# Six buffers in place of eight in the first mean stage, whole index lists, edge blocks, and two tiles of room before the gathers, in a four-layer graph network kernel

## The reference

```
q, k, v = x @ qW + qb, x @ kW + kb, x @ vW + vb
scores = sum(q[src] * k[dst]) / sqrt(16) + edge_attr @ eW + eb
out = segment_sum(v[src] * softmax_by_dst(scores), dst) @ oW + ob
x = layer_norm(x + out); h = gelu(layer_norm(x @ f1W + f1b)) @ f2W + f2b
x = layer_norm(x + h)
```

## Time and profile before

| | us |
|---|---|
| median of 3 runs | 6024.28 |
| lowest and highest run | 6012.01, 6027.09 |
| profiled execution, its own time | 6028.9 |
| its span in the trace | 6027.0 |

### The profile page before, as it was taken

How to read it: one execution, slowest core, us unless ns; L and a number is a source line. 1 busy time by engine, 2 the same in 40 slices (tenths; PEclk the granted TensorE clock), 3 DMA queues, 4 the chain that set the end, 5 groups by cost and what they waited for, 6 DMA issues and landing times. The chain is left out here.

```text
span 6027.0 us, 75672 instructions
## 1 busy us (share of the span) xinstructions
PE 4279.1 (71%) x16190; PEld 2524.1 (42%) x16190; DVE 4070.7 (68%) x13522; ACT 2924.8 (49%) x6388; POOL 3629.7 (60%) x3234
## 2 busy tenths in 40 slices
PE   6577759999997556546665679967996669836643
PEld 3244434444443333334443445534443334336643
DVE  6576659999997444457775676557665889836633
ACT  0466637777775010146665345534443446536643
POOL 4676558888885888735555660056104757855355
PEclk8788869999998777778887899988998899977877
DMA  6233323333332444456665675457545667757621
GB/s 214 66 85 80 73 70 99 99 99 99 99 99 78 62 62 63 54 141 196 193 190 162 185 211 146 131 160 214 164 141 147 176 159 211 197 162 227 183 78 54
DMA packets 767598, 802.43 MB, mean 133 GB/s; under 512 B 139632, under 2 KB 527800, under 8 KB 767018
## 3 DMA queue, kind: packets, MB, share of 16 engines
q1 hardware_dynamic: 405354, 393.44, 23.5%
q0 software_dynamic: 117504, 209.42, 15.0%
q10 hardware_dynamic: 244288, 194.72, 9.7%
HBM read 445.32 MB, written 351.92 MB: 132 GB/s over the span
## 5 line engine op out<-in xcount | busy, mean ns | idle before, releaser
L462 PE MATMUL gate_bank<-gate_ht,gate_whh 128*128 128x512 f32 x1764 | 874.6, 618 | 32.5 <-DVE gate_n L532 22.2
L925 POOL DMA_INDIRECT xh<-mean_xh,mean_pos_all x392 | 378.0, 964 | 349.0 <-DVE mean_xh L1027 158.9
L462 PEld LDWEIGHTS gate_bank<-gate_ht,gate_whh 128*128 128x128 f32 x1764 | 341.3, 202 | 413.0 <-issue 381.6
L2053 PE MATMUL back_ps_sums<-back_same,back_rows 128*128 128x512 f32 x400 | 289.5, 890 | 285.7 <-DMA back_rows<-x_a,back_idx 285.7
L151 POOL DMA_INDIRECT ffn_rows<-att_sums,ffn_idx x392 | 409.0, 1043 | 114.8 <-issue 106.3
L289 POOL DMA_INDIRECT gate_rows<-h_a,by_pos x200 | 195.8, 979 | 433.3 <-POOLq L117 327.3
L1494 PE MATMUL ffn_ps_f<-ffn_hg,ffn_f 128*128 128x512 f32 x784 | 407.1, 616 | 46.4 <-ACT ffn_hg L1671 46.4
L458 PE MATMUL gate_bank<-by_rank,gate_win 128*128 128x512 f32 x882 | 435.1, 593 | 0.0
L1487 PE MATMUL ffn_ps_u<-ffn_xs_t,ffn_up_w 128*128 128x512 f32 x784 | 387.2, 596 | 1.1 <-issue 1.1
L583 ACT ACTIVATE gate_z<-gate_bank,gate_b_rz 128x512 f32<-128x512 f32 x294 | 201.5, 686 | 351.0 <-PE gate_bank L462 221.0
L2034 POOL DMA_INDIRECT back<-back_out,back_dest x200 | 324.3, 1621 | 68.0 <-issue 60.1
(11 more groups left out here) (270 smaller groups left out, 11984.1 us busy)
## 6 DMA issues: line engine op xcount, KB each, us to landing
mean_x<-x_a SPq DMA_DIRECT2D x196, 256.0 KB
back<-blank ACTq DMA_DIRECT2D x99, 264.0 KB, 4.6
mean_rows<-back SPq DMA_DIRECT2D x98, 264.0 KB
hp<-mean_xh SPq DMA_DIRECT2D x98, 264.0 KB
gate_x<-xh SPq DMA_DIRECT2D x98, 264.0 KB
gate_hot<-hot_rows SPq DMA_DIRECT2D x100, 256.0 KB
ffn_x<-in_x_in SPq DMA_DIRECT2D x98, 256.0 KB
ffn_xr<-in_x_in SPq DMA_DIRECT2D x98, 256.0 KB
```

The source lines that it names most:

```text
L462: last = nc.tensor.matmul(bank_[:, :], whh[:, c * D:(c + 1) * D], ht[:, t.slot4, :], start=not inputs, stop=True)
L925: nc.gpsimd.indirect_dma_start(out=g["xh"][:, :], out_offset=bass.IndirectOffsetOnAxis(ap=pos_all[:, t.n, j:j + 1], axis=0), in_=xh[:, t.n ...
L2053: last = nc.tensor.matmul(ps_sums[t.slot][:, :], rows[:, t.slot4, j, :], same[:, t.slot, j, :], start=j == 0, stop=j == J - 1)
```

## The change

- First mean stage: the buffers `xh`, and the semaphores `scattered` and `h_stored`, go from 8 to FINISHED = 6. ACT's write of tile t waits for the scatter of tile t-6 (before: t-8).
- `SegmentSums.gather`, where the stage doesn't carry sums over (gate1, gate2 and mean3), and the gathers of attention: POOL waits for the use of tile t-2 (before: t-4), so two tiles of rows can be ahead of PE and not four. The buffers stay four.
- `gated_layer`: `hn` has four buffers (before: two), and the transposes of hn, what follows them on ACT and the stores come at item 3 (before: 2). In gate2 DVE's out and statistics come at item 3, rstd and shifts at 6 (5), apply, y's store and the scatter at 7 (6), the read back at 6 (5). Each layer's loops are one step longer.
- attention: SP loads the indices from a new input `edge_blocks` in which edge 128·j + p of a tile lies at partition p; turned rows are written to contiguous columns, L1206 reads contiguous columns of att, and `att_sums` is stored in pieces of 512 bytes in place of 2 KB.
- feed-forward: the whole list `ptr_dst` (98 tiles, 128 partitions, pieces of 16 bytes) is loaded once, first on SP's queue, in place of 98 loads; POOL's add a = rows + x goes to DVE, after z and ahead of the statistics; POOL's order in a step is gathers, xb, pow; and xh becomes `scalar_tensor_tensor` with the inverse root broadcast along the row as a second SBUF tensor, in place of `tensor_scalar`.

```
 SegmentSums.gather
-        wait(pool, self.summed, t.n - 3)
+        wait(pool, self.summed, t.n - 3 if self.carries else t.n - 1)
 gated_layer
-        d, hn = (f.sb(s, [P, 2, SUPER]) for s in ("d", "hn"))
+        d, hn = f.sb("d", [P, 2, SUPER]), f.sb("hn", [P, 4, SUPER])
 SP
-                if final and (t := item_at(5)) and t.has:
+                if final and (t := item_at(6)) and t.has:
 POOL
-                if final and (t := item_at(5)):
+                if final and (t := item_at(6)):
                     ln.rstd(nc, pool, t, y_done)
-                if final and (t := item_at(6)) and t.has:
+                if final and (t := item_at(7)) and t.has:
 PE
-                if t := item_at(2):
+                if t := item_at(3):
                     wait(pe, h_done, t.n + 1)
                     wait(pe, out_done, t.n)
...
-            over_items(2, step)
+            over_items(3, step)
 DVE
-                    wait(dve, h_turned, t.n - 1)
+                    wait(dve, h_turned, t.n - 3)
...
-                if final and (t := item_at(2)):
+                if final and (t := item_at(3)):
                     wait(dve, h_turned, t.n + 1)
                     wait(dve, x_loaded[t.slot4], 16 * (t.u4 + 1))
 back_mean_pass
-        xh = f.sb("xh", [P, 8, J, XH])
+        xh = f.sb("xh", [P, FINISHED, J, XH])
...
-                    wait(act, scattered[t.n % 8], 64 * (t.n // 8))
-                    wait(act, y_turned, t.n - 7)
+                    wait(act, scattered[t.n % FINISHED], 64 * (t.n // FINISHED))
+                    wait(act, y_turned, t.n + 1 - FINISHED)
 attention_pass
-                                 nm_tile(g["by_dst"], t)).then_inc(idx_loaded[t.slot4], 16)
+                                 g["edge_blocks"][t.n]).then_inc(idx_loaded[t.slot4], 16)
...
-                    wait(pool, rows_turned, t.n - 3)
+                    wait(pool, rows_turned, t.n - 1)
...
-                        nc.tensor.transpose(edge_columns(ps_send[:, :])[:, j, :], send[:, t.slot4, j, :], g["ident"][:, :])
+                        nc.tensor.transpose(ps_send[:, j * P:(j + 1) * P], send[:, t.slot4, j, :], g["ident"][:, :])
...
-                        last = nc.tensor.matmul(ps_out[:, j * D:(j + 1) * D], edge_columns(att[:, t.slot, :])[:, j, :],
+                        last = nc.tensor.matmul(ps_out[:, j * D:(j + 1) * D], att[:, t.slot, j * P:(j + 1) * P],
...
-                    act.dma_start(nm_tile(g["att_sums"], t), out[:, t.slot, :]).then_inc(stored[t.slot], 16)
+                    act.dma_start(part_tile(g["att_sums"], t.n, 0, D),
+                                  out[:, t.slot, :].rearrange("p (j d) -> p j d", j=J)).then_inc(stored[t.slot], 16)
 ffn_pass
-        idx = f.sb("idx", [P, 4, J], I32)
+        idx = f.sb("idx", [P, NT, J], I32)
...
+            sp.dma_start(idx[:, :, :], whole_list(g["ptr_dst"])).then_inc(idx_loaded, 16)
...
-                    wait_alone(sp, gathered[t.slot4], 64 * t.u4)
-                    sp.dma_start(idx[:, t.slot4, :], list_tile(g["ptr_dst"], t)).then_inc(idx_loaded[t.slot4], 16)
...
-                if t := tile_at(2):
-                    wait(pool, gathered[t.slot4], 64 * (t.u4 + 1))
-                    wait(pool, x_loaded[t.slot4], 16 * (t.u4 + 1))
-                    wait(pool, xh_done, t.n - 3)
-                    nc.gpsimd.tensor_tensor(flat(a[:, t.slot4, :, :]), flat(rows[:, t.slot4, :, :]),
-                                            flat(x[:, t.slot4, :, :]), ALU.add).then_inc(a_done, 1)
...
-                        last = nc.vector.tensor_scalar(xh[:, t.slot4, j, :], a[:, t.slot4, j, :],
-                                                       mv[:, root_slot(t, LN1), LN1, j, 0:1], inverse(t, LN1)[:, j:j + 1],
-                                                       ALU.subtract, ALU.mult)
+                        last = nc.vector.scalar_tensor_tensor(
+                            xh[:, t.slot4, j, :], a[:, t.slot4, j, :], mv[:, root_slot(t, LN1), LN1, j, 0:1],
+                            inverse(t, LN1)[:, j:j + 1].broadcast_to([P, D]), ALU.subtract, ALU.mult)
...
+                if t := tile_at(2):
+                    wait(dve, gathered[t.slot4], 64 * (t.u4 + 1))
+                    wait(dve, x_loaded[t.slot4], 16 * (t.u4 + 1))
+                    wait(dve, xh_done, t.n - 3)
+                    nc.vector.tensor_tensor(flat(a[:, t.slot4, :, :]), flat(rows[:, t.slot4, :, :]),
+                                            flat(x[:, t.slot4, :, :]), ALU.add).then_inc(a_done, 1)
```

More of the change, by code:

```diff
@@ L420, in step @@
                                  ).then_inc(back_loaded[t.m % 4], 16)
-            over_items(5 if final else 0, step)
+            over_items(6 if final else 0, step)
             if initial:
@@ L584, in step @@
                                          bias=b_rz[:, 1:2]).then_inc(z_done, 1)
-                if not final and (t := item_at(2)):
+                if not final and (t := item_at(3)):
                     wait(act, h_turned, t.n + 1)
@@ L602, in step @@
                     nc.scalar.activation(ht[:, t.slot4, :], ps_in[:, :], ACT.Copy).then_inc(ht_made, 1)
-                if final and (t := item_at(6)):
+                if final and (t := item_at(7)):
                     wait(act, y_done, t.n + 1)
                     act.dma_start(part_tile(x_out, t.tile, 0, D), y[:, t.slot, :, :]).then_inc(stored[t.slot], 16)
-            over_items(6 if final else 2, step)
+            over_items(7 if final else 3, step)
             for b in range(2):
                 act.wait_ge(stored[b], 16 * (NT // 2))
-                if not final:
-                    act.wait_ge(ht_stored[b], 16 * (NT // 2))
+            if not final:
+                for b in range(4):
+                    act.wait_ge(ht_stored[b], 16 * ((NT - b + 3) // 4))
 class Turn:
@@ L1437, in step @@
             def step(tile_at):
-                if t := tile_at(2):
-                    wait(pool, gathered[t.slot4], 64 * (t.u4 + 1))
-                    wait(pool, x_loaded[t.slot4], 16 * (t.u4 + 1))
-                    wait(pool, xh_done, t.n - 3)
-                    nc.gpsimd.tensor_tensor(flat(a[:, t.slot4, :, :]), flat(rows[:, t.slot4, :, :]),
-                                            flat(x[:, t.slot4, :, :]), ALU.add).then_inc(a_done, 1)
+                if t := tile_at(0):
+                    if t.n == 0:
+                        pool.wait_ge(idx_loaded, 16)
+                    wait(pool, a_done, t.n - 3)
+                    pool.nop(nofuse=True)
+                    for j in range(J):
+                        nc.gpsimd.indirect_dma_start(
+                            out=rows[:, t.slot4, j, :], out_offset=None, in_=g["att_sums"][:, :],
+                            in_offset=bass.IndirectOffsetOnAxis(ap=idx[:, t.n, j:j + 1], axis=0)
+                        ).then_inc(gathered[t.slot4], 16)
                 if t := tile_at(10):
```

60 lines of the change are left out of this document (31 added, 29 removed).

## The result

The changed kernel took 5861.08 us (median of 4 executions, 5828.97 to 5862.3) beside 6021.82 for the kernel before (6012.01 to 6027.09): a ratio of 0.9722, with a 95% interval of 0.9686 to 0.9758. The gain is 160.7 us where I had forecast 85; 5861 is at the very edge of my range (5860 to 6018). The profiled execution took 5861.81, its span is 5860.0.

A forecast was written before the change was run, and what follows sets the result against it. No engine bounds the whole kernel; POOL's own work sets the feed-forward step of 10.74 us. Terms -92 + 7 + 0 - 5 + 4 + 0 + 0 = -86 take 6028.9 to 5942.9, forecast as 5939 for the median; range 5860 to 6018.

The forecast's parts named there:

- Feed-forward, the step: Feed-forward stage: POOL's step of 10.74 us falls to 9.8 with PE late next, -92 us over 98 steps.
- The chance that POOL's remaining add would hold xh: Feed-forward rival: the xb add holds DVE's xh or z, stage gains only 21 us, time 6010; chance 0.10.
- The start: Start of the feed-forward stage: the whole index list goes ahead of the weights, +7 us, between 0 and +14.5.
- Attention: Attention: two tiles of room are enough for gathers, 0; shorter weight loads 0, at best -50; lower PE clock at worst +35.
- Segment sums' room: gate1, gate2 and mean3: two tiles of room before the gathers change nothing, 0, bounds -20 to +30 us.
- Bigger gain, the rival: First mean stage or stages like it: less room breaks up POOL's trains, 84 us more gained, time 5855; chance 0.12.
- Gated layers: Gated layers: PE's wait for hn goes, -5 us; one more step of drain a layer, +4 for the three.
- Slower by late x loads: Last gated layer rival: x loads over 4.9 us delay ACT; loads from 7.0 us give over 6042; chance 0.09.
- First mean stage: First mean stage: six buffers for eight cost 0, as POOL scatters a tile about as soon as it is done.

The follow-up runs named there:

- e7: The changed kernel with xh by the old tensor_scalar form again: 5925.19 us, ratio 0.9824 to the kernel before.
- e8: The kernel before with the new form of xh alone, both adds still on POOL: 6009.92 us beside 6028.14, ratio 0.9979.
- e14: The kernel before with six buffers of finished rows in the first mean stage alone: 6029.27 us beside 6026.5, ratio 1.0.
- e12: The changed kernel with six buffers of x in the last gated layer: 5895.71 us beside 6064.17 for the kernel before, ratio 0.9709.
- e18: The changed kernel with three tiles of room in attention: 5485.45 us beside 5583.56 for the kernel before, ratio 0.9824.
- e15: The changed kernel with one tile of room before attention's gathers: 5944.37 us, ratio 0.9856 to the kernel before.

## Why the prediction was right and wrong

- **Feed-forward, the step: mechanism right, one number mis-sized.** POOL's work did set the step. I had its new value, 9.48, by plain subtraction, and took 9.8 because PE's busy time gave 9.78. Measured: 9.42. The step of the prediction that failed here is the one from an upper bound to a value: "PE is late next. I take 9.8". PE's 9.78 held time in which it was not at work: its share shrank to 147.68 / 150 x 9.42 = 9.27 with the same instructions. (9.8 - 9.42) x 98 = 37 us were lost in this step. The stage gained 110 and not 98 x 1.32 - 7 = 122. The trace shows where the 12 are: of the 105 steps from the first pow to the last, the first five went from 9.2 to 8.1 us only and the last nine didn't change. In all the 105 went from 1086.0 to 971.2 us, and the first pow comes 5.0 later. So -92 + 7 = -85 were forecast for the stage, and -110 measured.
- **What held DVE.** The chance that POOL's remaining add would hold xh (0.10) didn't come true, and the reason given is borne out: xb lies under the statistics, and the maximum is 349 ns. But the new form isn't why: e7 shows the old one at 341 ns in the same place, and e8 shows the new one held when it stands beside the adds. I had priced the form at nothing on POOL's side; e7 shows it is worth 66 us there.
- **The start**: +7 forecast, +7.2 measured.
- **Attention: wrong.** I gave the room 0, with -50 in the bounds but for the weight loads. Measured: room -28 to -34 on the held kind, blocks 0. The step that failed is "two tiles ... are more than a gather needs: 0". It asked only whether less room starves PE, and not what a longer lead does to the others: on the held kind they take up the third tile about when POOL's first row of gathers ends, 75 us after the stage's start with four tiles and 54 with two.
- **Segment sums' room: wrong by the same step.** 0 forecast, -20 measured on the held kind, at the very edge of my -20 to +30, and +22 on the free kind, inside them. The starts of gate1, gate2 and mean3 came 11, 10 and 6 us sooner. My bound of -20 was drawn from the share of waits on L289's side and not from this, so that it holds is luck.
- **Bigger gain, the rival (0.12): right in kind.** It said that less room could break up POOL's trains and that the holds would get shorter; it priced 84 us more, from the holds of mean1. It came in attention, gate1 to mean3, where the room is what bounds a train, and not in mean1, where 8 or 6 buffers bound nothing (e14). What came is 48 to 54 us. (mean1 is also 728 us long by the table and not 697.)
- **Gated layers: one number mis-sized.** -5 + 4 forecast; -8 and -17 measured. I sized the term by the 27.3 us of waits in gate1; the gain is in gate2, where the same wait was 113.4.
- **Slower by late x loads (0.09): didn't come.** ACT does stand before the tails copy, as foreseen, 1.3 us in the step shown and up to 5.2 in the layer's first half. The load shown took 4904.00 - 4900.87 = 3.13 us, and from issue to the copy it is 4.3 us (median) in the first half and 3.2 in the second, under the 4.9 that cost nothing. e12 takes the wait away and gains nothing, so it is covered.
- **First mean stage**: 0 forecast, 0 measured.

The terms as measured on the held kind: -110 (ffn, start included), -28 to -34 (room in attention), -20 (room in the segment sums), -10 to -17 (gated): -168 to -181, beside -161 to -163 measured whole. Of the 75 us by which the forecast fell short, 25 are the ffn step, about 50 the two rooms and about 10 the gated layers; the terms measured alone add up to some 10 more than the whole.

That the time came out at the edge of the range is luck as well: the forecast had no term for what the room does, and on the free kind (e18, with three tiles in attention) the kernel gains 98 us, near the 85 forecast, with -110 in the ffn stage and a loss in gate1.

**What holds the engines** on such chips is not settled. Shown is: waits of over 1 us that end by "remote" come to 70 us in attention and 191 in mean1 in the kernel before, and there is none in any of the six runs on the free kind. The ffn stage, where 2.93 us of pow and 1.28 of xb part POOL's gathers, is as long on both kinds. So is the back stage, in which POOL does nothing but indirect DMAs (scatters of 1.63 us and gathers of 0.99, with pauses of 0.30) and sets the time itself; gathers and scatters without other work are thus not enough to hold the others for long. A shorter lead brings the start of a stage forward; one tile too few starves PE (e15). A pause of 0.96 us leaves most of the holds in place. Whether a pause as long as pow ends them wasn't tried on a chip of the held kind.

## What to carry to other kernels

An engine's new step by plain subtraction was here the better estimate than a neighbour's busy time: PE's busy time held 0.5 us a step (9.78 - 9.27) that went when its suppliers got faster, so such a sum is a weak upper bound. Ask of a buffer's depth not only whom less of it starves, but also what the engine that runs ahead does to the others while it does, and look for it at a stage's start, where nothing but the depth holds that engine back. And moving work between two engines that hold each other is worth more than its duration: 1.26 us less on POOL also took 1.9 us off DVE.

## What was not expected of the hardware

- Two kinds of chips for one program: 5584 to 5589 and 6022 to 6064 us, with the ffn and back stages equal to 4 us. The sign of a change (the room, +22 or -20) depends on the kind.
- On the slower kind the other engines take up a stage's third tile about when POOL's first row of gathers ends (75 us after attention's start with 48 gathers, 54 with 32), on the faster kind after 40 to 42 with either.
- The whole list of 98 x 128 pieces of 16 bytes holds the next load on SP's queue 6.34 us; on ACT's queue in mean1 the second such list held it 14.53.
- A DVE operation's form, with the same 340 ns, changes POOL's gathers from 1003 to 1200 ns on the mean (e7).
